# Side jobs of the matmul engine placed two parts at a time in every second quarter of the plan

## The reference, cut to what matters

```
x = x + attn_a(layernorm(x))     # 16 heads that share one score matrix: minus the distance of learned 3-d positions
x = x + ffn(layernorm(x))        # sigmoid(xr Wr) * (relu(xk Wk)^2 Wv); xr, xk mix a token with the one before it
x = x + attn_b(layernorm(x))     # 16 heads of size 16, causal softmax attention
x = x + ffn(layernorm(x))        # the same weights as above
```

## Time and profile before

| what | value |
|---|---|
| median of 3 runs | 2104.41 us (2093.51 to 2106.41) |
| profiled execution, its own time | 2109.85 us |
| its span in the trace | 2108.1 us |
| instructions in it | 32379 |
| PE busy | 1849.2 us, 88% |
| DVE busy | 1467.0 us, 70% |
| ACT busy | 1323.7 us, 63% |
| POOL busy | 728.2 us, 35% |
| mean granted clock of PE | 0.943 |

### The profile page before, as it was taken

One profiled execution on the slowest core, in us unless ns is written; L12 is line 12 of the kernel. 1 busy time (PEld: TensorE's weight loads), 2 busy tenths in 40 slices (PEclk: granted clock), 3 DMA queues, 4 the chain that ended last, 5 costly groups with the idle time before them and its releaser, 6 DMA issues. The chain is left out here.

```text
span 2108.1 us, 32379 instructions
## 1 busy us (share of the span) xinstructions
PE 1849.2 (88%) x9842; PEld 922.5 (44%) x9842; DVE 1467.0 (70%) x4288; ACT 1323.7 (63%) x2585; POOL 728.2 (35%) x879
## 2 busy tenths in 40 slices
PE   5677898889997999889998899979998899988986
PEld 4453443335543455434543355434544345322423
DVE  5576778767676677667786667766776677768642
ACT  3564355876569565776758665695657766455664
POOL 1342332234333253333443243333532334312313
PEclk8797899999998999999999899989999999989998
DMA  3006113111131112410132111311124101322000
GB/s 85 1 23 123 26 56 67 31 31 32 55 76 31 31 31 82 80 21 12 41 110 42 31 31 56 76 31 31 34 83 76 22 11 41 99 33 50 13 21 20
DMA packets 64346, 97.26 MB, mean 46 GB/s; under 512 B 15655, under 2 KB 58029, under 8 KB 58030
## 3 DMA queue, kind: packets, MB, share of 16 engines
q1 hardware_dynamic: 64174, 95.20, 20.2%
HBM read 61.09 MB, written 33.55 MB: 45 GB/s over the span
## 5 line engine op out<-in xcount | busy, mean ns | idle before, releaser
L973 ACT ACTIVATE pt<-exp_bank 128x512 f32<-128x512 f32 (+1 forms) x1216 | 698.9, 582 | 526.6 <-PE exp_bank L935 521.0
L989 DVE CUSTOM_DVE_ANT_0 max_bank<-max_bank,mask 128x128 f32<-128x128 f32 (+3 forms) x1024 | 501.8, 500 | 400.9 <-PE max_bank L922 386.4
L922 PE MATMUL max_bank<-ks,qs 96*128 96x512 bf16 (+3 forms) x1536 | 523.5, 346 | 85.9 <-DVE piece_max L992 44.9
L935 PE MATMUL exp_bank<-qs,ks 98*128 98x512 bf16 (+3 forms) x1536 | 515.4, 342 | 40.0 <-ACT pt L973 37.0
L992 DVE TENSOR_REDUCE piece_max<-max_bank 128x1 f32<-128x512 f32 x512 | 344.1, 686 | 94.4 <-PE max_bank L922 90.2
L954 PE MATMUL o_bank<-pt,v 128*17 128x512 f32 (+3 forms) x3072 | 334.1, 508 | 13.7 <-POOL pt L1011 11.0
L922 PEld LDWEIGHTS max_bank<-ks,qs 96*128 96x128 bf16 x1536 | 150.9, 99 | 399.5 <-DVE piece_max L989 140.9
L1011 POOL TENSOR_SCALAR_AFFINE_SELECT pt<-pt 128x512 f32<-128x512 f32 x256 | 171.5, 670 | 412.6 <-ACT pt L973 411.8
L935 PEld LDWEIGHTS exp_bank<-qs,ks 98*128 98x128 bf16 x1536 | 152.4, 100 | 236.0 <-ACT pt L973 118.5
L633 PE MATMUL side<-vp,p 128*128 128x260 f32 x576 | 171.4, 423 | 28.7 <-ACT p L560 21.0
L412 ACT ACTIVATE xh<-xs,shift,rstd 128x256 f32<-128x256 f32 x256 | 149.7, 596 | 47.8 <-POOL shift L401 47.8
(11 more groups left out here) (119 smaller groups left out, 2348.4 us busy)
## 6 DMA issues: line engine op xcount, KB each, us to landing
parts_dram<-parts SPq DMA_DIRECT2D x64, 384.0 KB, 2.6
qs<-parts_dram SPq DMA_DIRECT2D x192, 128.0 KB, 7.2
ks<-parts_dram SPq DMA_DIRECT2D x32, 384.0 KB, 4.7
xs<-in_L_attn_a_x_dram SPq DMA_DIRECT2D x16, 512.0 KB, 4.2
ks<-parts_dram SPq DMA_DIRECT2D x32, 256.0 KB, 5.4
out_dram<-xs SPq DMA_DIRECT2D x16, 512.0 KB, 3.1
ks<-parts_dram SPq DMA_DIRECT2D x32, 128.0 KB, 5.8
qs<-neg_maxT SPq DMA_DIRECT2D x64, 8.0 KB, 1.9
```

What stands on the lines that cost most here:

```text
L922: pe.matmul(max_bank[u % MAX_BANKS][:, 0:k1 - k0], qs[r][0:KROWS, j, P * tile:P * (tile + 1)], ks[r][0:KROWS, j, k0:k1], start=True, stop= ...
L935: mm = pe.matmul(exp_bank[k % EXP_BANKS][:, (q1 - q0) * slot:(q1 - q0) * (slot + 1)], ks[r][:, j, P * kt:P * (kt + 1)], qs[r][:, j, q0:q1] ...
L973: act.activation(pt[:, e % 2, j + 1 - heads:j + 1, 0:w], exp_bank[k % EXP_BANKS][:, 0:heads * w].rearrange("p (j n) -> p j n", j=heads), A ...
L989: dve.tensor_tensor_reduce(scores, scores, mask[:, HALF - w:HALF], 1.0, LOWEST, ALU.add, ALU.max, piece_max[:, j, m:m + 1]).then_inc(max_f ...
```

## The change

The planner's step for the side parts is replaced. Before, each quarter takes the first part of the list, if it is due and, for the first part of a job, if a bank is free. Now, from quarter 0 on, an even quarter takes no part, and an odd one takes up to two. To make room for the second, a part may be placed before it is due: by one quarter if it is the first of its job, by up to two otherwise. Below quarter 0 (the first 224 quarters, which hold no attention) nothing changes. The row jobs keep their quarters.

```
-        if parts:
+
+        for _ in range(1 if u < 0 else 2 * (u % 2)):
+            if not parts:
+                break
             at, key, k, last = parts[0]
             regained = max(0, shift - max(0, at - before) // 4)
-            if at + regained <= u and (k > 0 or min(free) <= u):
-                parts.pop(0)
-                before, shift = at, max(regained, u - at)
-                late.append((at, shift))
-                if k == 0:
-                    bank[key] = free.index(min(free))
-                    free[bank[key]] = NEVER
-                    quarters[key] = []
-                quarters[key].append(u)
-                if last:
-                    emptied[key] = free[bank[key]] = u + delay[key]
+            if at + regained > u + (u >= 0) * (1 if k == 0 else 2) or k == 0 and min(free) > u:
+                break
+            parts.pop(0)
+            before, shift = at, max(regained, u - at)
+            late.append((at, shift))
+            if k == 0:
+                bank[key] = free.index(min(free))
+                free[bank[key]] = NEVER
+                quarters[key] = []
+            quarters[key].append(u)
+            if last:
+                emptied[key] = free[bank[key]] = u + delay[key]
         u += 1
```

## The result

The changed kernel takes 2216.0 us (median of 4 runs, 2213.2 to 2218.7), against 2105.4 us before: 1.054 times as long (95% interval 1.050 to 1.058), that is 5.4% slower. One of the four runs behind the 2105.4 us fell in a slower state of the chip, at 2414.7 us, and the ratio is taken without it. The profiled execution took 2214.8 us, its span is 2213.0 us, 104.9 us more than before. Lines of the changed kernel from `place()` on are four higher: L926 is the max matmul that was L922, L446 the transposition, L745 keys, L619 values1.

What follows compares the result with a forecast made beforehand. Most of a turn was taken as PE issuing without pause. Late inputs add 14.5 us a turn, less 3.5 absorbed: 11 us over 7.2 turns, 79 us, giving 2183 us; 8 in 10 from 2110 to 2245 us.

Steps and rivals of the forecast that it cites:

- the waits were to grow to some 75, 35 and 20 us: Sign of being right: PE's waits on xh, pb and xt grow from 23, 9 and 3 us.
- PE's work unchanged, no switch cost: PE in dense quarters: a pair takes 2.50 us before and after; saving taken as 0, bounded by -31 us.
- a sign of a switch cost: Sign of being wrong: a pair of quarters under 2.4 us, with the waits at early parts unchanged.
- Transpositions: PE at `tr` behind ACT's last xh: five waits of 1.3 us and two of 0.5, 7.5 us a turn.
- Keys: PE at `keys` behind DVE's second xk: four waits of 1.0 us, 4.0 us a turn.
- Values1: PE at a half's first `values1` behind ACT's copy to xt: two waits of 1.5 us, 3.0 us a turn.
- The absorbed part: A quarter of the 15 us of bank waits a turn shrinks while PE waits: 3.5 us a turn off the sum.
- no cost: PE at `receptance`, `products` and `project`: still 5 or more quarters behind their inputs, cover 6 us and over.
- This costs nothing, but also gives nothing: Two score banks fill 0.38 us apart; DVE's 1.4 us of reductions fit PE's 2.1 us away: no cost, no gain.
- The clock rival: 11 waits over 1 us a turn drop PE's clock: 119 us more, 2300 us; chance 0.07.

Runs made afterwards that it cites:

- all_up: Changed kernel with DVE's second xk and ACT's xh rows 2 to 4 up one quarter, att1 copies to xt up one or two; 1.0207 times the kernel before.
- even_pairs: Changed kernel with its pairs of parts in even quarters instead of odd ones, early parts still allowed; 1.022 times the kernel before, 2140 us.
- due_pairs: Changed kernel, pairs still in odd quarters, but from quarter 0 on every part is read as planned one quarter later; 1.044 times the kernel before, 2194 us.
- xh_down: Changed kernel with ACT's last xh row one quarter later where it stood in an even quarter; 1.088 times the kernel before, 2284 us.

## Why the prediction was right, and where not

The forecast was 2183 us, a 79 us loss; measured are 2216 us and 105 us of span (111 us by the medians). The sign and the main mechanism, parts that come before their input, were right: taking the three waits away gave back 3.3 of the 5.4%. The other 2.1% belong to terms that the forecast had at nothing. Of its signs, the waits were to grow to some 75, 35 and 20 us; they grew to 62, 37 and 10 us.

- *PE's work unchanged, no switch cost*: right. In the changed kernel a pair of quarters without a wait, with 512- and 256-column scores, takes 1070.44 to 1072.83 us, 2.39 us; score starts of 0.22 and 0.11 us, twice, and 2 x 0.86 us make 2.38. It lies under the 2.4 us that the forecast named as a sign of a switch cost only because one of the two scores has 256 columns here, and had 384 in the quarter that its 2.50 us came from.

```profile
1070.44 0.38 PE L926 MATMUL max_bank<-ks,qs 96*128 96x512 bf16 x1
...
1070.78 0.38 PE L926 MATMUL max_bank<-ks,qs 96*128 96x512 bf16 x1
...
1071.11 1.89 PE L759 MATMUL side<-wrT,pb 128*128 128x256 f32 x8
1072.83 0.38 PE L926 MATMUL max_bank<-ks,qs 96*128 96x512 bf16 x1
```

- *Transpositions*: forecast 7.5 us a turn, 54 us in 7.2 turns. Measured 39.5 us of more wait, and 38 more waits x 0.17 us of drain, 46 us; the removal gave 37.6 us of span (26 us by the ratios).
- *Keys*: forecast 29 us. Measured 28.0 + 26 x 0.17 = 32 us of wait; the removal gave 19 us (17 us by the ratios), with a part of the wait left.
- *Values1*: forecast 22 us, all for `xt`. Measured 7.7 us more on `xt` and 6.6 us on DVE's `on`. Half of the mechanism was another: a side bank not yet emptied. all_up took 19 us off by the ratios and 23 us of span, more than these waits; its mean clock is 0.945 against 0.941, up to 10 us, and executions of one kernel differ by as much.
- *The absorbed part*: this is the term that was mis-sized. I took 3.5 us a turn, 25 us, off the sum, because ACT and DVE catch up while PE waits. The three bank waits are 117.0 us before and 116.4 us after, so nothing was absorbed. Without it the sum is 14.5 x 7.2 = 104 us, beside 105 measured. That it fits so well is luck, since transpositions and values1 were lower, and other things fill the gap: up to 13 us of clock, and a term that isn't in the forecast at all, side banks not yet emptied when a part comes early. Beside `on` these are `project` (L829), 6.7 us where there was none, and `positions` (L604), 7.8 us instead of 0.9. For `project` I had looked only at the distance to its input and written "no cost".
- *"This costs nothing, but also gives nothing"* of the two score banks: right for the changed kernel (117.0 and 116.4 us) and for all_up (118.0 us), not for pairs placed otherwise: the two max banks cost 101 us in even_pairs and 117 us in due_pairs, against 80. The versions with pairs and the least waits for inputs are still 1.7 to 2.9% slow, by score banks, side banks and clock together; no run takes these three apart. I had checked a mean load, 1.4 us of reductions in 2.1 us, and not what else stands between two reductions in DVE's stream.
- *The clock rival*: 0.940 against 0.943, so at most 13 of the 105 us, where the rival had 119 us. That its mechanism exists, xh_down shows: no fall after the waits of 1.23 to 1.29 us, one after 8 of 12 of 1.61 us. The Trainium skill, TensorE: Matmul & The Clock Gate, section "A second HAM failure mode: psum-queue depth-cycling", has idle times between groups of matmuls as a cause of clock changes; the trace agrees for xh_down, and doesn't for the changed kernel's dense stretch, at 1.00 with waits of 1.2 to 1.3 us.

## What to carry to other kernels

When work of a saturated engine is regrouped, look not at the work but at the distance, in time, between each input's writer and its reader, and at what stands between them: a quarter that became 0.38 us long is no distance at all. Move the writer with the reader; in the kernel before that cost 0.4%, and here it gave back more than half of the loss. Ask of an early part also whether its output buffer is free: a wait for a side bank looks like one for an input, and moving the writer leaves it whole. And even spacing can be worth something by itself where another engine has only two buffers: the mean load says it fits, and the order of that engine's stream decides. Whether it does depends on the placement, as due_pairs and all_up show.

## What the runs showed of the hardware that I had not expected

- The clock makes long waits dearer than short ones. xh_down added 32 us of wait and 74 us of span, with the granted clock going from 0.940 to 0.919: a fall after all 18 transposition waits of 2.10 to 2.26 us, after none of the 24 of 1.23 to 1.29 us.
- In the changed kernel one `xk` of DVE took 1.22 us, where it took 0.75 us before (both rows above and in the earlier trace rows). POOL ran a 128x512 addition beside it, which in the kernel before began only at 1009.63, after it. The median of this instruction is 0.75 us in both kernels, its mean went from 0.81 to 0.88 us. The trace points to POOL as the cause. L679 and L686 have 19 rows that began with 0.6 us or more of such a POOL instruction (a TENSOR_TENSOR of 256 to 512 columns) still to run. All 19 end 0.55 us after POOL's does, here at 1060.56 after 1060.01, and last 1.20 to 1.52 us. Of 22 rows where POOL's began after DVE's, 21 took 0.74 to 0.77 us. So DVE stood until POOL was through. 12 of the `xk` last 1.20 to 1.22 us in this way; no run moves POOL's instruction away.
